# GpSimd's products and sums of the state scan, two states to an instruction: 128x1024 in place of 128x512

## The reference

```python
# the feed-forward part, H = 1024
gate, up = jnp.split(jnp.einsum('bsd,hd->bsh', x, wq_gu), 2, axis=-1)
h = jax.nn.silu(gate) * up
hn = rms_norm(h)                       # needs the sum of h*h over H
return jnp.einsum('bsh,dh->bsd', hn, wq_p)

# the scan: 256 channels (e), 16 states (n), 4 x 256 time steps
def step(state, xs):
    d_t, B_t, C_t, u_t = xs
    dA = jnp.exp(d_t[..., None] * A)
    state = state * dA + (d_t * u_t)[..., None] * B_t[:, None, :]
    y_t = jnp.einsum('ben,bn->be', state, C_t)
    return (state, y_t)
y = y + D[None, :, None] * u
```

## Time and profile before

| | |
|---|---|
| time, median of 3 runs | 476.12 us (475.71 to 476.35) |
| the profiled execution | 480.81 us, span 479.1 us, mean granted clock 0.881 |
| PE, DVE, ACT, POOL busy, share of the span | 73%, 71%, 48%, 69% |
| POOL's products of C and state (L561) | 64, 80.8 us in all |
| POOL's pair sums (L567) | 32, 40.7 us in all |
| POOL's `add_square` (L573) | 16, 20.5 us in all |
| loads of C's rows | 64 of 256 KB, median 3.2 us to landing |

### The profile page before, as it was taken

How to read it: one execution, slowest core, us unless ns; L and a number is a source line. 1 busy time by engine, 2 the same in 40 slices (tenths; PEclk the granted TensorE clock), 3 DMA queues, 4 the chain that set the end, 5 groups by cost and what they waited for, 6 DMA issues and landing times.

```text
span 479.1 us, 6716 instructions
## 1 busy us (share of the span) xinstructions
PE 350.8 (73%) x1795; PEld 238.6 (50%) x1805; DVE 338.3 (71%) x772; ACT 228.4 (48%) x443; POOL 328.8 (69%) x279
## 2 busy tenths in 40 slices
PE   4738924698888889888538246988888888888870
PEld 2324712244444455444227235777676667676650
DVE  2999799799989988989776874544554544554464
ACT  1799959677677777674133101332322322233210
POOL 3211637699999999999621363787878777887860
PEclk9996865699999989999865557999999998999995
DMA  8900003357666333332000222888888888874557
GB/s 251 367 7 7 1 0 98 106 157 207 181 172 216 116 111 125 116 112 88 0 0 1 110 68 67 212 211 197 211 197 210 195 197 195 212 175 88 95 67 257
DMA packets 54441, 64.72 MB, mean 135 GB/s; under 512 B 6098, under 2 KB 42754, under 8 KB 54290
## 3 DMA queue, kind: packets, MB, share of 16 engines
q1 hardware_dynamic: 43264, 47.59, 32.6%
q0 software_dynamic: 9984, 16.78, 18.1%
q10 hardware_dynamic: 1170, 0.08, 0.2%
HBM read 53.36 MB, written 11.08 MB: 134 GB/s over the span
## 4 chain that ended last, share of the span: by engine, by line
POOL 22%; PE 19%; DVE 17%; ACT 16%; issue 14%; DMA 9%; SPq 1%; another core or an unknown queue 1%; DVEq 0%; POOLq 0%; ACTq 0%
POOL sums L621 8%; PE bank L1161 5%; POOL ssm L610 4%; POOL ssm L561 4%; DVE ssm L1366 4%; DVE bank L1361 3%; DMA ssm<-routed,idx 3%; POOL ffn L573 3%; DMA arena<-in_L_ffn_w_gate_up 3%; ACT L809 3%; ACT ssm L788 3%; PE bank L1145 2%; PE bank L1126 2%; PE bank L1139 2%; PE bank L1033 2%
## 5 line engine op out<-in xcount | busy, mean ns | idle before, releaser
L621 POOL DMA_INDIRECT sums<-ssm,idx x48 | 79.2, 1649 | 20.9 <-issue 13.1
L1466 DVE COPY ssm<-bank 128x256 f32<-128x256 f32 x64 | 27.1, 423 | 80.2 <-PE bank L1126 59.4
L561 POOL TENSOR_TENSOR ssm<-ssm,bc_buf 128x512 f32<-128x512 f32 x64 | 80.8, 1273 | 4.1 <-DVE ssm L1366 4.1
L610 POOL DMA_INDIRECT ssm<-routed,idx x64 | 65.4, 1021 | 26.6 <-issue 16.2
L1366 DVE TENSOR_TENSOR_SCAN ssm<-ssm,bank 128x512 f32<-128x512 f32 x64 | 78.1, 1221 | 2.4 <-DVE bank L1361 0.2
L1161 PE MATMUL bank<-arena,ssm 128*128 (+1 forms) x256 | 57.8, 350 | 8.7 <-issue 4.2
L862 ACT ACTIVATE ssm<-bank 128x96 f32<-128x96 f32 x64 | 16.0, 250 | 89.5 <-PE bank L1161 75.3
L1145 PE MATMUL bank<-ssm,xin 128*128 128x256 bf16 x384 | 52.1, 274 | 0.1
L1161 PEld LDWEIGHTS bank<-arena,ssm 128*128 128x128 f32 x256 | 42.3, 199 | 16.2 <-issue 13.0
L998 PE MATMUL bank<-ssm,ident 128*128 128x512 f32 x64 | 36.4, 650 | 18.8 <-POOL ssm L567 17.1
L855 ACT ACTIVATE ssm<-bank 128x256 f32<-128x256 f32 x64 | 24.5, 383 | 49.2 <-PE bank L1139 32.9
(11 more groups left out here) (215 smaller groups left out, 689.5 us busy)
## 6 DMA issues: line engine op xcount, KB each, us to landing
bc_buf<-c_rows SPq DMA_DIRECT2D x64, 256.0 KB, 3.2
arena<-in_L_ffn_gate_proj SPq DMA_DIRECT2D x32, 192.0 KB
arena<-in_L_ffn_up_proj SPq DMA_DIRECT2D x32, 192.0 KB
arena<-in_L_ffn_down_proj SPq DMA_DIRECT2D x32, 192.0 KB
sums<-zero_f SPq DMA_DIRECT2D x1, 2304.0 KB, 13.9
arena<-in_L_ffn_w_gate_up SPq DMA_DIRECT2D x1, 2048.0 KB, 13.9
routed<-xw SPq DMA_DIRECT2D x1, 1280.0 KB, 4.4
x_res<-in_x SPq DMA_DIRECT2D x1, 1024.0 KB, 8.7
```

The source lines that it names most:

```text
L561: pool.tensor_tensor(prod[:, k % 4, :], hs[:, k % 3, :], C_buf[:, k % NCB, :], ALU.mult).then_inc(s.prod_ok, 1)
L610: pool.indirect_dma_start(out=xe[:, k, :], out_offset=None, in_=routed, in_offset=bass.IndirectOffsetOnAxis(ap=idx2[:, k, 0:1], axis=0)).t ...
L621: pool.indirect_dma_start(out=sums, out_offset=bass.IndirectOffsetOnAxis(ap=idx2[:, k, 1:2], axis=0), in_=ye[:, k, :], in_offset=None, com ...
```

## The change

POOL's products are made two steps at a time, as one 128x1024 instruction, and the two pairs of a unit are added as one 128x1024 instruction: block 0 to block 2 and block 1 to block 3. C's rows come in pairs, 512 KB to a DMA, to one of two halves of `C_buf`. The scans have four blocks in place of three, in two pairs; the scan of step k waits for the product of the pair two before. PE sums the two results of a unit one after the other, in the next unit. In the last unit POOL makes its last two products narrow and leaves out the sum, and PE sums four single products. On ACT, `keep_y` goes behind the Square. Arithmetic is the same up to the order of the sum.

```diff
-            def product(k):
-                pool.wait_ge(ld_C[k % NCB], 16 * (k // NCB + 1))
-                pool.wait_ge(s.scan_ok, k + 1)
-                if k % 2 == 0 and k >= 4:
-                    pool.wait_ge(s.pair_ok, k // 2 - 1)
-                if k % 2 == 1 and k >= 5:
-                    pool.wait_ge(s.sum_ok, k // 2 - 1)
-                pool.tensor_tensor(prod[:, k % 4, :], hs[:, k % 3, :], C_buf[:, k % NCB, :], ALU.mult).then_inc(s.prod_ok, 1)
-            def add_pair(j):
-                pool.wait_ge(s.prod_ok, 2 * j + 2)
-                a = (2 * j) % 4
-                pool.tensor_tensor(prod[:, a + 1, :], prod[:, a + 1, :], prod[:, a, :], ALU.add).then_inc(s.pair_ok, 1)
+            def product(q, first=0, steps=2):
+                pool.wait_ge(ld_C[q % 2], 16 * (q // 2 + 1))
+                pool.wait_ge(s.scan_ok, 2 * q + first + steps)
+                a, b = 2 * (q % 2) + first, 2 * (q % 2) + first + steps
+                if q % 2 == 0 and q >= 2:
+                    pool.wait_ge(s.pair_ok, q // 2)
+                if q % 2 == 1 and q >= 3:
+                    pool.wait_ge(s.sum_ok, q - 1)
+                pool.tensor_tensor(prod[:, a:b, :], hs[:, a:b, :], C_buf[:, a:b, :], ALU.mult).then_inc(s.prod_ok, 1)
+            def add_pairs(f):
+                pool.wait_ge(s.prod_ok, 2 * f + 2)
+                pool.tensor_tensor(prod[:, 2:4, :], prod[:, 2:4, :], prod[:, 0:2, :], ALU.add).then_inc(s.pair_ok, 1)
...
-            for f in range(UNITS):
-                product(4 * f)
-                product(4 * f + 1)
-                add_pair(2 * f)
-                product(4 * f + 2)
+            for f in range(UNITS - 1):
+                product(2 * f)
                 if f > 0:
                     add_square(f - 1)
                 if f == 9:
                     rms(0)
-                product(4 * f + 3)
-                add_pair(2 * f + 1)
+                product(2 * f + 1)
+                add_pairs(f)
+            product(PAIRS - 2)
+            add_square(UNITS - 2)
+            product(PAIRS - 1, 0, 1)
+            product(PAIRS - 1, 1, 1)
             add_square(UNITS - 1)
...
+                src = bass.AP(tensor=src.tensor, offset=src.offset + th * 512, ap=[[0, P], [TOK, 2], [1, 512]])
+                sp.dma_start(C_buf[:, 2 * (q % 2):2 * (q % 2) + 2, :], src).then_inc(ld_C[q % 2], 16)
...
+                for q in (2 * f, 2 * f + 1):
+                    if q + 2 < PAIRS:
+                        sp.wait_ge(s.prod_ok, q + 1)
+                        c_load(q + 2)
...
-                if f and f % 4 == 0:
-                    keep_y(f // 4 - 1)
                 act.wait_ge(s.h_ok, f + 1)
                 if f > 0:
                     act.wait_ge(s.acc_ok, f + 2)
                 act.activation(hsq, hT[f % 2], ACT.Square).then_inc(s.hsq_ok, 1)
+                if f and f % 4 == 0:
+                    keep_y(f // 4 - 1)
...
-                if f > 0:
-                    sum_states(2 * f - 1)
                 if 4 * f + 4 < STEPS:
                     broadcast(4 * f + 4)
...
-                sum_states(2 * f)
+                if f > 0:
+                    sum_pairs(f - 1)
                 if 4 * f + 5 < STEPS:
                     broadcast(4 * f + 5)
...
             project(UNITS - 1)
-            sum_states(2 * UNITS - 1)
+            n = 2 * UNITS - 1
+            sum_states(UNITS - 1, ((s.prod_ok, n), (s.prod_ok, n), (s.prod_ok, n + 1), (s.prod_ok, n + 2)), (0, 1, 2, 3))
...
-                if k >= 3:
-                    dve.wait_ge(s.prod_ok, k - 2)
-                dve.tensor_tensor_scan(hs[:, k % 3, :], dA[:, k % 3, :], x[:, :], 0.0, ALU.mult, ALU.add).then_inc(s.scan_ok, 1)
+                if k >= 4:
+                    dve.wait_ge(s.prod_ok, k // 2 - 1)
+                dve.tensor_tensor_scan(hs[:, k % 4, :], dA[:, k % 3, :], x[:, :], 0.0, ALU.mult, ALU.add).then_inc(s.scan_ok, 1)
```

More of the change, by code:

```diff
@@ L54 @@
 NB = 3
-NCB = 4
+PAIRS = STEPS // 2
 def part(ap, *dims, offset=0):
@@ L243, in build @@
         ssm = sb("ssm", [P, 4, 2, TOK])
[L244 to L247, removed]
+        scan_buf = part(ssm[:, 0, 0, 0:1], (512, 11), (1, 512))
+        dA, hs = scan_buf[:, 0:3], scan_buf[:, 3:7]
+        prod = scan_buf[:, 7:11]
+        C_buf = part(bc_buf[:, 2, 0:1], (512, 4), (1, 512))
         y_buf = bc_buf[:, 0:2]
@@ L375, in build @@
         s = Semaphores(sem)
-        ld_C = [sem(f"ld_C{k}") for k in range(NCB)]
+        ld_C = [sem(f"ld_C{k}") for k in range(2)]
         ld_moe = [sem(f"ld_moe{k}") for k in range(2)]
@@ L412, in _, with c_load @@
             sp.wait_ge(s.delta_sb, 4)
[L414 to L416 removed]
+            def c_load(q):
+                th, h, n, t = of_step(2 * q)
                 src = c_rows[n:n + 1, :]
[L418 to L419 removed]
+                src = bass.AP(tensor=src.tensor, offset=src.offset + th * 512, ap=[[0, P], [TOK, 2], [1, 512]])
+                sp.dma_start(C_buf[:, 2 * (q % 2):2 * (q % 2) + 2, :], src).then_inc(ld_C[q % 2], 16)
             def moe_load(b, e):
@@ L428, in moe_load @@
                              down_proj[bass.ds(e, 2)].rearrange("e i d -> i e d")).then_inc(ld_moe[b], 16)
-            for k in range(NCB):
-                c_load(k)
+            for q in range(2):
+                c_load(q)
             for f in range(UNITS):
@@ L990, in broadcast, with sum_states @@
                 pe.matmul(bank[(5, 6, 4)[k % NB]][:, :], sel[0:XR, n, :], B_parts[0:XR, t], start=True, stop=True).then_inc(s.bb_ps, 1)
[L992 to L999, removed]
+            def sum_states(f, ready, parts):
+                p = f // 4
+                for done, a in zip(ready, parts):
+                    pe.wait_ge(*done)
+                    if f % 4 == 0 and a == parts[0] and p:
+                        pe.wait_ge(s.y_sb, p)
+                    pe.matmul(bank[3][:, :], ident[:, :], prod[:, a, :], start=f % 4 == 0 and a == parts[0], stop=False, skip_group_check=True).then_inc(s.sum_ok, 1)
+                if f % 4 == 3:
                     pe.wait_ge(s.skip_ok, 2)
@@ L1002, in sum_states, with sum_pairs @@
                     pe.matmul(bank[3][:, :], skip_diag[:, p % 2, :], u[:, p % 2, t], start=False, stop=True, skip_group_check=True).then_inc(s.y_ps, 1)
+            def sum_pairs(f):
+                sum_states(f, ((s.pair_ok, f + 1), (s.pair_ok, f + 1)), (2, 3))
             def project(f):
@@ L1514, in rows @@
                 dve.wait_ge(s.idx_step, 5 * a + 5)
-            dve.wait_ge(s.prod_ok, STEPS)
+            dve.wait_ge(s.prod_ok, PAIRS + 1)
             dve.wait_ge(s.c_ident, 8)
```

## The result

The changed kernel took 472.40 us (median of 20 runs, 468.94 to 473.84), the kernel before 476.58 us in the same comparison. The ratio is 0.9905, 95% interval 0.9889 to 0.9921: 4.5 us less, between 3.8 and 5.3. Forecast were 469.8 us and 6.3 us less, range 467.3 to 474.3.

A forecast was written before the change was run, and what follows sets the result against it. The prediction took POOL's own instructions in the state loop as the bound, with DVE next. Loop -4.8, wait in unit 9 +1.1 and tail -2.6 gave -6.3 us, so 476.12 became 469.8 us, range 467.3 to 474.3.

The forecast's parts named there:

- POOL sets the pace: State loop: nothing makes POOL wait, its unit takes 8.83 us; DVE's 7.98 us a unit is the next bound.
- The wide instruction costs what the undisturbed `du` row says: POOL's 128x1024 instructions: 2.37 us long, 2.29 to the next start, 2.45 where the next one waits for it.
- Rivals 1 and 2: Wide instruction saves nothing (474.9 us, 8%); or it costs the `du` rows' mean, 2.81 us (488.5 us, 4%).
- the slow `du` row: First of two wide POOL products making `du`: 3.26 us, while DVE's L1336 ran; that cause is absent in the loop.
- The unit, 8.42 us: One loop unit on POOL with wide products and sum: 8.42 us against 8.83, 0.41 us less.
- the hand-over from sum to product: POOL's wide sum to the next product, which waits for it: 2.45 us from start to start.
- The wait in unit 9, 1.1 us: POOL's `product(21)` waits 1.1 us for PE, which runs zero and project at half clock, 3.72 us.
- The tail, 2.6 us: Behind the last product: without the pair sum, PE's squares end 3.3 us after it instead of 5.9, gaining 2.6 us.
- rival 3: C's row pair lands late, at 7.0 us instead of 4.7, lengthening 7 units by 0.95 us: 476.5 us, chance 5%.
- The median behaves like the profile's span: Whole program: the runs' median is 4.69 us below the profiled 480.81 us, so 476.12 - 6.3 = 469.8 us.

The follow-up runs named there:

- i1: The changed kernel, where in six units POOL adds only one block to one and PE sums the left-over product by itself; 465.16 us.
- p1: The changed kernel with a third pair of product blocks, so the even product no longer waits for the sum just ahead; 467.64 us.
- i3: The changed kernel with single sums in all odd units up to 13 and a third pair of product blocks; 465.21 us.
- w1: The changed kernel with the wide pair sum replaced by two 128x512 sums, products still wide; 474.10 us.
- n1: The changed kernel with each wide product issued as two 128x512 products, sums still wide; 474.49 us.
- c0: The changed kernel again, no edit, for a second profile; 472.19 us.
- b1: The kernel before again, no edit, for a second profile; 476.30 us.

## Why the prediction was right, step by step

- *POOL sets the pace.* Shown, by i1 and p1: less POOL work shortens the loop by nearly as much (5.6 us for six times 1.1, 3.1 to 3.3 for fifteen times 0.21), until 7.98 us a unit, where DVE takes over as the prediction had it (i3).
- *The wide instruction costs what the undisturbed `du` row says*, 2.29 to the next start. It is 2.31 to 2.32, and 2.44 before a sum that waits. The fixed cost is 0.14 to 0.15 us (w1, n1). Rivals 1 and 2 are out. DVE's rows in the tail of the changed kernel, with one of POOL, and one of DVE from before show what the disturbed row was about:

```profile
73.74 1.22 DVE L1333 TENSOR_TENSOR bc_buf<-bc_buf 128x1024 f32<-128x1024 f32 x1
...
218.61 5.67 DVE L1402 SCALAR_TENSOR_TENSOR x_res<-xw,coef,x_res 128x256 f32<-128x256 f32 x4
...
227.31 1.04 POOL L514 TENSOR_TENSOR rstd<-rstd,mhalf 128x4 f32<-128x4 f32 x1
227.32 1.67 DVE L1402 SCALAR_TENSOR_TENSOR x_res<-xw,coef,x_res 128x256 f32<-128x256 f32 x4
```

Its four `x_res` updates, two SBUF inputs each, took 5.67 us beside POOL's last products and squares, one for each POOL instruction, and 1.67 us beside POOL's 128x4 operation. POOL's narrow products beside them took 1.45 us in place of 1.27. In the 14 units no such DVE operation runs and no product was slowed (2.35 to 2.37 us each). The prediction put the slow `du` row (73.90) down to L1336, which started 1.09 us behind it. L1333, also with two SBUF inputs, was running when it started and ended at 74.96, 1.06 us later; the row was 0.89 us longer than the other. L1336 then ended 1.1 us behind the product (78.24 and 77.16) and took 3.25 us, where the one at 72.60 took 1.23. These times fit POOL held by L1333, and L1336 held by POOL; the prediction's conclusion, that the cause is absent in the loop, stands.

Beside POOL's 128x4 operation, which lasted 1.04 us (227.31 to 228.35), DVE's updates were not held: the first two ended at 227.81 and 228.20, while it ran. What holds them beside the others, no run shows.
- *The unit, 8.42 us.* It is 8.50. The term that was mis-sized is the hand-over from sum to product, 2.52 us in place of 2.45 (the step from product to square adds 0.02 to 0.03); 14 x 0.08 = 1.1 us.
- *The wait in unit 9, 1.1 us.* This step failed: there was none. From `zero` to `gate_up` PE took 2.40 us (2.68 in c0) in place of 3.72, since the stretch at half the clock fell for the most part on the sums ahead of `zero`. Where it did fall there, 3.65 us in w1, POOL waited as the prediction says, but 0.6 us and not 1.1. That this error and the one before cancel is luck: the loop gained 3.4 to 3.55 us where 4.8 - 1.1 = 3.7 was forecast.
- *The tail, 2.6 us.* 2.8 us against the profile that I had, as forecast. But that profile's tail of 6.2 us is one of two values. Against 4.8 us the tail gains 1.4. The forecast asked for 1.8 us more than was measured; the step that it rests on most is this one, which took one execution's tail as the rule (1.2 us of the 1.8). What ends the new tail is also not PE, done at T + 2.8 in place of T + 3.3, but DVE's statistics, at T + 3.3 as the prediction had them. The 1.4 us are POOL's: from its last product to the end of its last `add_square` were 2.81 us with the pair sum (b1) and are 1.41 without.
- *C's landing* (rival 3) was never near: 4.9 us at worst, and the added 256 KB cost 0.3 to 0.4 us, where I took 1.16, an estimate from the traffic of one stretch (226 GB/s from 100 to 104 us).
- *The median behaves like the profile's span.* Roughly. Outside loop and tail 13 of the 14 profiles spent 333.3 to 335.9 us, the first of before 338.0. That scatter, 2.5 us, is more than half of the gain, so the span of one profile could not give it; loop and tail could.

Loop and tail of the profiles give 5.0 us less (139.8 against 134.8, before with the short tail) or 6.2 (with the long one); the measured 3.8 to 5.3 fits the short tail. That most timed executions have the short one is argued, not shown.

What stays open: why a hand-over costs 0.13 us from product to sum, 0.21 from sum to product and 0.27 where the product waits for one semaphore more (i1: 121.51 to 123.01 is 1.50 against 1.23). The number of waits rises along with it. The number alone costs nothing: in i3 the first product of an odd unit waits for four semaphores too, none of them for the sum just ahead, and starts 2.30 us behind it (111.67 to 113.97). What further waits add to one on the instruction just ahead, no run separates.

## What to carry to other kernels

Where an engine is busy without a gap, count its instructions and its hand-overs: here 0.14 us for each POOL instruction and 0.13 to 0.2 us for each that waits for the one just ahead, and take the price of a wider one from any row of that shape that ran undisturbed. Then look at what stands behind the loop, and at every engine there: with the last unit left wide the whole gain went back into the tail, and in the new tail it is DVE that ends last, not PE. Profile a kernel more than once before a forecast takes a stretch of it for granted: this tail had two lengths, some 1.3 us apart. When the bound is one engine and a neighbour has room, move one operation in some rounds only: on top of the wide loop this gave 7.0 us more (i1, 465.2 us, 2.3% under the kernel before), where the whole change had given 4.5. What it gives without the wide loop was not run.
